# Queries and keys placed tile to tile, the first two batches' turned scores in another bank pair, and new engine orders, in a fused conditional transformer kernel

## The reference, cut to what matters

```python
# 0: per-batch adapter; its weights come from cond through two large matrices (Wdd, Wdu)
x = x + relu(x @ Wd_b.T + bd) @ Wu_b.T + bu
# 1: layer norm, times weight plus bias, with a bias per batch
# 2: modulated transformer block, 16 heads of 16
h = layernorm(x) * g1 + b1
q, k, v = split(h @ W_qkv.T + b_qkv)
o = softmax(q @ k.T / 4) @ v            # per head, 256 x 256 scores
x = x + (o @ W_o.T + b_o) * a1
h = layernorm(x) * g2 + b2
x = x + (gelu_tanh(h @ W_f1.T + b_f1) @ W_f2.T + b_f2) * a2
# 3: gated layer with quantised activations and ternary weights
h = x * (cond @ norm_w.T + 1) * rsqrt(mean(x * x) + eps)
val, gate = split(h @ up_w.T)
y = act_quant(val * gelu(gate)) @ weight_quant(down_w).T + x
```

## Time and profile before

| | us |
|---|---|
| median of 3 runs | 881.86 |
| lowest and highest | 879.83, 883.41 |
| the profiled execution | 881.95 |
| its span | 880.1 |
| TensorE busy | 798.5 (91%) |
| VectorE busy | 555.9 (63%) |
| ScalarE busy | 554.7 (63%) |
| GpSimd busy | 324.1 (37%) |

### The profile page before, as it was taken

One profiled execution on the slowest core, in us unless ns is written; L12 is line 12 of the kernel. 1 busy time (PEld: TensorE's weight loads), 2 busy tenths in 40 slices (PEclk: granted clock), 3 DMA queues, 4 the chain that ended last, 5 costly groups with the idle time before them and its releaser, 6 DMA issues.

```text
span 880.1 us, 16405 instructions
## 1 busy us (share of the span) xinstructions
PE 798.5 (91%) x6108; PEld 634.1 (72%) x6108; DVE 555.9 (63%) x1063; ACT 554.7 (63%) x844; POOL 324.1 (37%) x398
## 2 busy tenths in 40 slices
PE   6753377999999999999999999999999999999977
PEld 4103256778787878787878788888788887877664
DVE  1313856677767768585858585858586867675424
ACT  1012343668695858685867777676868676867652
POOL 1003423253534344443434352625252535232330
PEclk9855767999999999999999999999999999999998
DMA  9989633434243332425151515141524423220000
GB/s 344 386 325 355 260 127 109 145 106 136 97 136 112 128 121 99 150 86 163 69 179 50 195 49 170 56 171 59 168 77 153 143 96 106 106 94 9 25 13 12
DMA packets 56207, 118.50 MB, mean 135 GB/s; under 512 B 6112, under 2 KB 11616, under 8 KB 53424
## 3 DMA queue, kind: packets, MB, share of 16 engines
q1 hardware_dynamic: 56128, 117.46, 38.6%
HBM read 82.23 MB, written 34.16 MB: 132 GB/s over the span
## 4 chain that ended last, share of the span: by engine, by line
PE 77%; DVE 5%; issue 5%; ACT 4%; POOL 4%; DMA 4%; SPq 1%; POOLq 0%; DVEq 0%; ACTq 0%
PE bank L528 41%; PE pair_s L692 6%; PE pair_t L528 5%; PE bank L789 3%; PE pair_s L680 3%; PE bank L703 3%; DMA hyp<-in_hyper 2%; PE pair_s L658 2%; PE bank L781 2%; PE pair_t L680 2%; PE bank L596 2%; PE bank L602 1%; DVE nmax L1180 1%; PE pair_t L658 1%; DVE hd L1248 1%
## 5 line engine op out<-in xcount | busy, mean ns | idle before, releaser
L1398 POOL TENSOR_TENSOR G_lo<-G,G_hi 128x512 fp32r<-128x512 f32 x64 | 81.9, 1293 | 117.6 <-ACT G_hi L922 117.6
L528 PE MATMUL bank<-wup_hi,hD_hi 128*128 128x512 f32 x256 | 110.5, 432 | 3.8 <-POOL hD_lo L1371 3.1
L528 PE MATMUL bank<-wup_lo,hD_hi 128*128 128x512 f32 x256 | 101.8, 397 | 0.0
L528 PE MATMUL bank<-wup_hi,hD_lo 128*128 128x512 f32 x256 | 101.7, 397 | 0.0
L902 ACT ACTIVATE Pr<-pair_s 128x1024 f32<-128x1024 f32 x64 | 65.7, 1027 | 44.3 <-PE pair_s L680 44.0
L1408 POOL TENSOR_TENSOR x<-x,gated 128x512 f32<-128x512 f32 x16 | 20.4, 1274 | 165.6 <-DVE gated L1238 165.6
L1180 DVE TENSOR_REDUCE nmax<-pair_s 128x4 f32<-128x1024 f32 x64 | 77.9, 1217 | 4.5 <-PE pair_s L658 4.2
L1180 DVE TENSOR_REDUCE nmax<-pair_t 128x4 f32<-128x1024 f32 x64 | 77.7, 1214 | 0.0
L528 PE MATMUL bank<-wf_hi,G_hi 128*128 128x256 f32 x256 | 76.9, 300 | 0.9 <-ACT G L917 0.8
L1204 DVE STREAM_TRANSPOSE oq<-pair_s 128x512 f32<-128x512 f32 x32 | 22.9, 717 | 78.8 <-PE pair_s L692 78.8
L949 ACT ACTIVATE gl<-bank,rsD 128x512 f32<-128x512 f32 x64 | 43.7, 683 | 45.2 <-PE bank L528 44.9
(11 more groups left out here) (192 smaller groups left out, 2251.7 us busy)
## 6 DMA issues: line engine op xcount, KB each, us to landing
hyp<-in_hyper SPq DMA_DIRECT2D x16, 1024.0 KB, 10.0
Qp<-qk_scratch SPq DMA_DIRECT2D x64, 256.0 KB, 4.7
Kp<-qk_scratch SPq DMA_DIRECT2D x64, 256.0 KB, 4.6
qk_scratch<-q_hi SPq DMA_DIRECT2D x16, 512.0 KB, 2.8
qk_scratch<-k_hi SPq DMA_DIRECT2D x16, 512.0 KB, 3.2
tC<-rows_scratch SPq DMA_DIRECT2D x16, 384.0 KB, 4.5
xT_t<-in_xT SPq DMA_DIRECT2D x16, 256.0 KB, 4.5
x_t<-in_x SPq DMA_DIRECT2D x16, 256.0 KB, 4.6
```

Of the source, the lines that this page charges most:

```text
L528: mm = pe.matmul(dst, l, r, start=first and i == 0, stop=last and i == 2)
L1398: pool.tensor_tensor(G_lo[:, 2 * i:2 * i + 2, :], G[:, 2 * i:2 * i + 2, :], G_hi[:, 2 * i:2 * i + 2, :].bitcast(F32), ALU.subtract).then_i ...
```

## The change

It does five things.

1. **Tile to tile.** The DRAM scratch for queries and keys is gone. SyncE places each part straight into every fourth partition of `Qp` or `Kp`, 32 partitions and 64 KB at a time: 8 DMAs for `q_hi` (`A.qh0`), 8 for `k_hi` (`A.kh0`), 4 for `q_lo` (`A.ql0`), 4 for `k_lo` (`A.kl0`), and two DMAs that bring the zeros back into the fourth rows of the first pairs, 26 in place of 12. `heads_in[j]` now counts all parts. The evictions no longer wait for stores to be done, but for the scores of the batch before.
2. **Another bank pair.** For batches 0 and 1 the turned scores of pairs 0 to 3 go to `pair_u` (banks 6 and 7), so `B.t0` may run before `B.m1`. Pairs 0 to 3 share it: each waits for the exponential of the one before.
3. **Weight splits in pieces** of 1024 columns on VectorE, `w_f2` in four on GpSimd, each a step of its own; the up weights' high part in two; wqkv's low part waits for GpSimd's `nb1`.
4. **Prologue.** `second` is filled after the stores, not between the chunks; wqkv is loaded after the first gates; and TensorE runs matmuls whose result nobody reads (`keep_busy`): one behind each of chunks 6 to 14, 6 behind the last, 15 behind the first `A.up`, 4 behind the first `A.ht`.
5. **New orders** for all five engines, in all turns.

```diff
+        pair_u = ctx.enter_context(nc.psum_tensor("pair_u", [P, 2, HALF], F32))
+        bank += [pair_u[:, 0, :], pair_u[:, 1, :]]
+
+        def turned(p, b):
+
+            return pair_u if b <= 1 and p < GP else pair[p % 2]
...
-            def store_part(w, rows, part, stored):
-
-                dst = qk_scratch[w, :, rows, :]
-                src = part[:, :, :].rearrange("p a b -> p (a b)").unsqueeze(1).to_broadcast([P, dst.shape[1], 2 * L])
-                sp.dma_start(dst, src.bitcast(F32)).then_inc(stored, 16)
...
+            def place(dst, part, rows, par):
+
+                for j in range(4):
+                    for r in rows:
+                        sp.dma_start(dst[r:P:4, par, 2 * j:2 * j + 2, :].bitcast(F32), part[32 * j:32 * j + 32, :, :].bitcast(F32)).then_inc(heads_in[j], 16)
...
+                    elif (stage, what) == ("A", "qh"):
+                        past(sp, pe_t, PE_T, f"t{NP - 1}", a, 2)
+                        if a == 0:
+                            sp.wait_ge(planes_out, 16 * 9)
+                        for half in range(2):
+                            sp.dma_start(Qp[64 * half + 3:64 * half + 8:4, par, :, :].rearrange("p c n -> p (c n)").bitcast(F32),
+                                         none_scratch.rearrange("q j n -> q (j n)")).then_inc(heads_in[0], 16)
                         sp.wait_ge(act_a, at(ACT_A, "qhi1", a))
-                        store_part(0, slice(0, 2), q_hi, qh_out)
+                        place(Qp, q_hi, (0, 1), par)
...
+            def second_rows():
+                for c in range(NCH):
+                    sp.dma_start(second[8 * c:8 * c + 8, :], gen[1:P:NB, c, :]).then_inc(second_in, 16)
...
+            def keep_busy(n):
+
+                for _ in range(n):
+                    pe.matmul(bank[7][:, 0:D], ident, wo[:, 0, :], start=True, stop=True)
+
             for c in range(6, NCH):
                 generate(c)
+                keep_busy(1 if c < NCH - 1 else 6)
...
                 def b_s(n):
-                    pe.wait_ge(heads_in[n], 32 * b + 32)
+                    pe.wait_ge(heads_in[n], (128 if n == 0 else 96) * (b + 1))
...
-                        if p == 0:
+                        if b <= 1 and p <= GP + 1:
+                            if 0 < p < GP:
+                                pe.wait_ge(act_t, at(ACT_T, f"exp{p - 1}", b))
+                            elif p == GP:
+                                pe.wait_ge(dve_m, at(DVE_M, f"t{NG - 1}", b))
+                                pe.wait_ge(dve_o, at(DVE_O, "tr0", b))
...
+            def up_weights(q):
+                k, cols = q // 2, slice(FF * (q % 2), FF * (q % 2 + 1))
+                dve.wait_ge(act_w, at(ACT_W, f"up{k}", 0))
+                dve.tensor_tensor(wup_lo[:, k, cols], wup_raw[:, 2 * FF * k + FF * (q % 2):2 * FF * k + FF * (q % 2 + 1)],
+                                  wup_hi[:, k, cols].bitcast(F32), ALU.subtract).then_inc(dve_w, 1)
...
 FULL = {
     "SP": """
-        -1: A.kl1 D.y1 A.kl2 A.ql3 A.kl3 0: B.m0 A.load A.qs B.m1 A.ks D.y0 A.ql0 A.kl0 1: C.tc 0: A.ql1 A.ql2""",
+        -1: A.qh0 B.m1 A.kh0 A.kl0 D.y0 0: C.tc -1: A.ql0 D.y1 0: B.m0 A.load""",
```

More of the change, by code:

```diff
@@ L463, in turn @@
                     if stage == "W":
-                        {"store": store_rows, "f": f1_rows, "up": up_rows, "late": late_weights}[what]()
-                    elif (stage, what) == ("A", "qs"):
-                        previous_loaded(a)
+                        {"second": second_rows, "store": store_rows, "zero": zero_rows, "f": f1_rows, "up": up_rows, "late": late_weights}[what]()
+                    elif (stage, what) == ("A", "qh"):
[5 more added lines that the diff above has]
+                                         none_scratch.rearrange("q j n -> q (j n)")).then_inc(heads_in[0], 16)
@@ L491, in turn @@
+                        place(Kp, k_lo, (1,), par)
                     elif (stage, what) == ("B", "m"):
@@ L679, in b_t @@
                                 lo = 64 * half
-                                mm = pe.matmul(pair[p % 2][:, half, k * L:(k + 1) * L], Kp[lo:lo + KR, 1 - par, p, k * P:(k + 1) * P],
+                                mm = pe.matmul(turned(p, b)[:, half, k * L:(k + 1) * L], Kp[lo:lo + KR, 1 - par, p, k * P:(k + 1) * P],
                                                Qp[lo:lo + KR, 1 - par, p, :], start=True, stop=True)
@@ L960, in turn @@
                     if stage == "W":
[L961 removed]
+                        {"qkv": qkv_weights, "fa": f1_weights, "ftwo": f2_weights}[what]() if what != "upper" else up_weights(n)
                     elif stage == "A":
```

249 lines of the change are left out of this document (129 added, 120 removed).

## The result

The change makes the kernel slower: median 910.61 us (907.46 to 917.17), against 881.4 for the kernel before, ratio 1.034 with a 95% interval of 1.0275 to 1.0404. The profiled execution took 907.46 us with a span of 905.7, which is 25.6 more than the 880.1 of the profile before. Forecast were 877 us, with a range from 868 to 889.

A forecast was written before the change was run, and what follows sets the result against it. TensorE, busy 91% of 880.1 us, was taken as the bound, with gains only before 181 us. Head -10.4, waits behind tC +4.6 and +0.8 elsewhere sum to -5.0: 877 us, range 868 to 889.

The forecast's parts named there:

- the price e: SyncE's time to issue one 32-partition placing, everywhere: taken as 0.43 us, with 0.57 as upper bound.
- no bound: Steady turns: the placings cost SyncE 11.5 us in a turn of 45.8 us, so they do not limit it.
- the slower rival: SyncE's issues become the bound at e = 0.57, in head, turn 3 and turn 15: 887.5 us; chance 0.28.
- First scores of batch 0, forecast 95.0: Head: SyncE's unbroken issues end at 92.1, a load lands 2.9 us later; scores at 95.0 against 96.91, -1.9 us.
- From there to the first turned scores, forecast 11.5: Head: 21.6 us shrinks by 4.6 (weight split) and 6.1 (other bank pair), +0.6 left; turned scores at 106.5.
- on to turn 2, forecast 18.6: Four turned pairs in series take about 7.4 us, then about 11.2 us; turn 2 starts at 125.1, 10.4 earlier.
- Turn 2, forecast as long as before: Turn 2: first maximum ahead of a norm +0.5, second turned four -0.5, so turn 3 also starts 10.4 us earlier.
- the -10.4 of the sum: Head's gain: turn 2, and so turn 3, start 10.4 us earlier than in the kernel before.
- Steady turns, forecast +0.5 each: Turns 5 to 13: q low's placings wait behind tC's load, so TensorE waits 0.5 us, nine times: +4.6 us.
- Turns 3 to 5, forecast +0.3 and 0.5 behind tC: Turn 3's last keys, issued after the loads, are tight: +0.3 us; from turn 5, q low behind tC costs 0.5.
- turns 14 and 15, forecast +0.5: Tail: turn 15's queries come last in the list, +0.5 us.
- it decides from e = 0.45: Turn 3, in the slower rival: keys land at 539.1 + 20e against a need at 548.0, late from e = 0.45.
- The halved head: Rival: keep-busy matmuls at the low clock take 15.4 us, losing 3 to 5 us of head gain: 881 us; chance 0.12.

The follow-up runs named there:

- row_planes: row_ql_first with the zero planes of Qp laid in 2 DMAs of 128 source partitions instead of 8 of 32; 871.5 us.
- stores_act: row_planes with the prologue's four 1 MB stores on ScalarE's queue instead of SyncE's; 867.79 us.
- change_ql_first: The change, still with 24 placings, with q low placed ahead of the output and tC in turns 5 to 13; 909.22 us.
- scratch_rest: The change without tile to tile: queries and keys go through the DRAM scratch as before, 4 stores and 8 loads a batch; 872.14 us.
- one_per_row: The change with reordered query and key weight columns, so one 128-partition DMA serves all four quarters: 6 placings a batch instead of 24; 879.67 us.
- row_ql_first: one_per_row with q low placed ahead of the output and tC, instead of behind tC, in turns 5 to 13; 874.49 us.

## Why the prediction was wrong, by its steps

**The step that failed is the price e**, SyncE's time to issue one placing. It was taken as 0.43 from the nearest rows in number of partitions, the loads and the 16-partition store. Those have DRAM at one end. The earlier trace rows has two rows with a tile at both ends, the copy into `cur` with 0.57 and the maxima's DMA with 0.62, not the "only copy" of the prediction; they were the nearest in kind, and the placings cost 0.594, 0.62 with the pause between two. The sum also left the pause out of the cheap price: two loads in a row are 0.48 apart.

**The second step that failed is "no bound".** The prediction set a batch's issues against a turn of 45.8 us. By that working even 0.62 would have been no bound (24 x 0.62 + 1.2 = 16). What counts is the stretch from q high's being ready to the next turn's first scores: there SyncE's list takes 18.4 us, and TensorE waits for its end in nearly every turn. SyncE's issues as the bound was the slower rival's mechanism, with a chance of 0.28, but that too charged the steady turns nothing beyond the 0.5 us for tC, and its 887.5 was too low by 23 us.

The span was forecast 5.0 us shorter and came out 25.6 longer, a miss of 30.6: 14.6 up to turn 3's first scores, 6.3 in turns 3 to 5, 3.8 in the eight turns from 6 on, 4.7 in turns 14 and 15, and 1.2 at the end.

*First scores of batch 0, forecast 95.0, measured 101.48.* The list started earlier than I had it, at 56.7 rather than 60.7 (56.0 to 58.9 in the other runs with this head): up to 4 us of gain that I had missed. The copies into second no longer stand between the chunks and wqkv is loaded later; no run parts the two. But up to the first placing of q low it took 42.6 us against my 31.0: the zero planes 7.3 against 3.9, stores and second 18.5 against 14.7, the 20 placings 12.6 against 8.6, and smaller ones. From that placing to the scores it then took 2.1 us, where I had 3.3. row_planes and stores_act take two of these out and get 2.0 and some 4.5 us back from the gates to the first scores.

*From there to the first turned scores, forecast 11.5, measured 11.76; on to turn 2, forecast 18.6, measured 17.5.* These terms held in sum: the weight split out of the way, the turned scores directly behind, the four pairs in series. The closeness is in part luck, as change_ql_first took 2.4 us more for the same lists. Turn 2 started at 130.72, later than the 125.1 by the first scores' delay, less 1.

*Turn 2, forecast as long as before.* It failed. Even in scratch_rest, without any placing, from its start to the next first scores it takes 48.6 us, not 45.3. TensorE is busy 39.45 us in it against 37.76, at a clock of 0.82 against 0.89, which is half of the difference, and it waits twice 1.1 us for exponentials of the shared pair. With the same order of TensorE and a clock of 0.89, row_planes takes 46.7 and stores_act 46.8. That the -10.4 of the sum came out at turn 3 of scratch_rest (-10.45) is two misses against each other: turn 2 starts 13.7 earlier there, and takes 3.3 longer. In the change it takes 54.3: besides that it waits 2.92 and 2.42 us for low keys.

*Steady turns, forecast +0.5 each for q low behind tC, measured +0.99.* The mechanism and size were right by themselves: one_per_row has +0.49, and row_ql_first loses it. The other half is SyncE's 18.4 us of issues behind q high, which push tC 1.1 us behind `gated`. The two are not parted in the change itself, where moving q low ahead of tC won nothing.

*Turns 3 to 5, forecast +0.3 and 0.5 behind tC, measured +7.1; turns 14 and 15, forecast +0.5, measured +5.2.* The trace shows the same kind of wait, for low keys or low queries, in lists where placings stand behind the maxima's DMA or last. With the same lists and a quarter of the issues (one_per_row) these stretches are 137.8 and 91.3 us, against 145.5 and 96.8, and the loss is gone. The rival's own working for turn 3, "it decides from e = 0.45", was right; but it charged the lateness once, where the next turn's issues start only when its queries are there, so nothing is caught up.

*The halved head* did not come about: TensorE's 15 calls behind `A.up` (30 instructions) took 7.84 us, not the 15.4 I had counted from a row at the low clock, and the queries were ready 10 us before SyncE reached them.

## What to carry to other kernels

Count what a list of DMA issues costs its engine as the number of issues times the spacing of two issues of the same kind, and take that spacing from a row with the same two ends (tile or DRAM) and the same stride; the number of partitions or bytes was no guide here. Then set the sum against the time from when the data is ready to when it is needed, not against the length of a turn. Replacing a few large transfers through DRAM by many small ones between tiles saves bytes that may cost nothing and spends issues that do: arrange the layout, here the order of the weights' columns, so that one DMA does the work of four. And price two parts of a change together as well as apart: a part that removes waits can lay bare the cost of the other, here +7.8 and -8.9 that came to +29.2.
